# Group 1's attention scores by query, and part of the late rotation on VectorE, in a transformer block of fp32 products

## The reference

```python
h = ada_rms(x, time_emb, ln1_w, ln1_tw)          # x * rsqrt(mean(x^2)) * w * (1 + t @ tw.T)
q, k, v = h @ Wq.T, h @ Wk.T, h @ Wv.T           # 8 query heads, 1 key/value head of 32
q, k = apply_rope(q, pos_ids), apply_rope(k, pos_ids)   # q * cos + rotate_half(q) * sin
attn = softmax(einsum('bkgsd,bktd->bkgst', qg, k) / sqrt(32))
x = x + (attn @ v) @ Wo.T
h = ada_rms(x, time_emb, ln2_w, ln2_tw)
out = x + (silu(h @ Wg.T) * (h @ Wu.T)) @ Wd.T   # 1024 inner features
```

## Time and profile before

| | us |
|---|---|
| median of three runs (111.22, 111.94, 111.80) | 111.80 |
| profiled execution, time | 111.32 |
| its span | 109.5 |
| TensorE busy | 102.8 (94%) |
| VectorE busy | 70.2 (64%) |
| ScalarE busy | 50.5 (46%) |
| GpSimd busy | 61.9 (57%) |
| TensorE's granted clock, every 5 us of the span | 1.00 |

### The profile page before, as it was taken

One profiled execution on the slowest core, in us unless ns is written; L12 is line 12 of the kernel. 1 busy time (PEld: TensorE's weight loads), 2 busy tenths in 40 slices (PEclk: granted clock), 3 DMA queues, 4 the chain that ended last, 5 costly groups with the idle time before them and its releaser, 6 DMA issues. The chain is left out here.

```text
span 109.5 us, 2352 instructions
## 1 busy us (share of the span) xinstructions
PE 102.8 (94%) x748; PEld 95.4 (87%) x748; DVE 70.2 (64%) x176; ACT 50.5 (46%) x136; POOL 61.9 (57%) x92
## 2 busy tenths in 40 slices
PE   5979989999998999998999989999999999999990
PEld 4858758769898999988999979999999999999990
DVE  1476976889999947347998435479984354666311
ACT  5082868778626365213662326145524522444300
POOL 1006696399899979968189982252552410555500
DMA  2899999700000000000020000000200000200011
GB/s 72 141 354 411 293 363 416 313 4 6 0 0 3 6 0 0 0 0 9 0 96 0 0 0 6 3 0 0 96 6 0 0 0 0 99 6 0 0 48 48
DMA packets 3707, 7.66 MB, mean 70 GB/s; under 512 B 624, under 2 KB 1648, under 8 KB 3696
## 3 DMA queue, kind: packets, MB, share of 16 engines
q1 hardware_dynamic: 3552, 7.51, 20.0%
q10 hardware_dynamic: 144, 0.01, 0.1%
HBM read 6.47 MB, written 1.05 MB: 69 GB/s over the span
## 5 line engine op out<-in xcount | busy, mean ns | idle before, releaser
L1104 POOL TENSOR_TENSOR hf_l<-hf,hf_h 128x256 fp32r<-128x256 f32 x32 | 24.0, 751 | 24.4 <-ACT hf_h L985 24.4
L415 PE MATMUL ps_gu<-h_h,wgu_h 128*128 128x256 f32 x120 | 25.2, 291 | 0.0
L415 PE MATMUL ps_gu<-h_h,wgu_l 128*128 128x256 f32 x120 | 23.9, 280 | 0.0
L415 PE MATMUL ps_gu<-h_l,wgu_h 128*128 128x256 f32 x120 | 23.9, 280 | 0.0
L978 ACT ACTIVATE th<-ps_gu 128x256 f32<-128x256 f32 x32 | 12.2, 381 | 23.3 <-PE ps_gu L415 22.9
L764 DVE SCALAR_TENSOR_TENSOR sg<-th,ps_gu 128x256 f32<-128x256 f32 x32 | 13.2, 411 | 11.9 <-ACT th L978 11.6
L415 PEld LDWEIGHTS ps_gu<-h_h,wgu_h 128*128 128x128 f32 x120 | 18.8, 188 | 0.3
L985 ACT ACTIVATE hf_h<-hf 128x256 fp32r<-128x256 f32 x32 | 13.2, 412 | 11.4 <-DVE hf L773 11.3
L415 PEld LDWEIGHTS ps_gu<-h_l,wgu_h 128*128 128x128 f32 x120 | 18.4, 188 | 0.0
L415 PEld LDWEIGHTS ps_gu<-h_h,wgu_l 128*128 128x128 f32 x120 | 18.3, 188 | 0.0
L773 DVE TENSOR_TENSOR hf<-sg,ps_gu 128x256 f32<-128x256 f32 x32 | 13.5, 420 | 1.0
(11 more groups left out here) (142 smaller groups left out, 198.3 us busy)
## 6 DMA issues: line engine op xcount, KB each, us to landing
wgu<-in_w_gu SPq DMA_DIRECT2D x4, 512.0 KB, 9.4
xt<-in_xT SPq DMA_DIRECT2D x4, 256.0 KB, 6.6
wd<-in_w_d SPq DMA_DIRECT2D x2, 512.0 KB, 12.6
out_x<-xk SPq DMA_DIRECT2D x3, 256.0 KB, 2.2
pb<-in_pack_b SPq DMA_DIRECT2D x1, 576.0 KB, 6.2
xk<-in_x_tok SPq DMA_DIRECT2D x2, 256.0 KB, 8.1
xk<-in_x_tok SPq DMA_DIRECT2D x1, 512.0 KB, 11.5
wqkv<-in_w_qkv SPq DMA_DIRECT2D x1, 320.0 KB, 5.3
```

Of the source, the lines that this page charges most:

```text
L415: mm = pe.matmul(ps_gu[:, slot % RING, part, cols], w[:, m, span(part * KH + k, 1, P)], h[:, k, cols], start=(step == 0 and k == 0), stop= ...
L1104: pool.tensor_tensor(hf_l[:, m], hf[:, m], hf_h[:, m].bitcast(F32), ALU.subtract).then_inc(hf_lo, 1)
```

## The change

Group 1's scores are computed by query, as group 0's are: the turned form and VectorE's flip stay for groups 2 and 3 alone. With that TensorE turns group 1's `prob` (four transposes between chunks 4 and 5) and ScalarE copies it, where VectorE turned it. For groups 2 and 3 VectorE forms `rot_a` and the sum `qk_rot`, between `low_x2` and `turn_qk` at the end of stages 0 and 1; GpSimd keeps `rot_b`. In the first attention `spread_v` goes ahead of tile 1's maximum, and ScalarE's copy of `probT` ahead of `high_gu(1)`. In stages 1 and 2 chunk 6's product (`hidden`) goes ahead of the attention sum.

```diff
@@ TensorE
-                    if g:
+                    if g > 1:
                         mm = pe.matmul(bank_s(g, c0, n)[:, span(c, 1, HG * P)], keys, qkT[:, c, 0:HG * P],
...
             def turn_probs(g, c, n):
                 pe.wait_ge(prob_ready, done(g, c, n))
-                if c:
+                if g:
+                    pe.wait_ge(h2_lo, CT * g)
+                elif c:
                     pe.wait_ge(below_ready, c)
...
             gate_up(0, 4)
+            turn_probs(1, 0, CT)
             gate_up(0, 5)
@@ VectorE
-                return by_row(flip[:, :] if g else bank_s(g, c, n)[:, span(c, n, HG * P)])
+                return by_row(flip[:, :] if g > 1 else bank_s(g, c, n)[:, span(c, n, HG * P)])
...
+            def late_rotate_a(g):
+                ts = slice(g * CT, (g + 1) * CT)
+                dve.wait_ge(table_ready, 3 * (g - 1))
+                q = qkv_sb[:, ts, 0:QK].rearrange("p c (h d) -> p c h d", d=HD)
+                a = rot_a[:, :, :].rearrange("p c (h d) -> p c h d", d=HD)
+                dve.tensor_tensor(a, q, cos[:, ts].rearrange("p t u d -> p t (u d)").unsqueeze(2)
+                                  .broadcast_to([P, CT, HEADS + 1, HD]), ALU.mult).then_inc(late_a, 1)
+
+            def late_add(g):
+                dve.wait_ge(late_b, 2 * (g - 1))
+                dve.wait_ge(late_a, g - 1)
+                dve.wait_ge(qkT_ready, CT * g)
+                dve.wait_ge(kbd_ready, CT * g)
+                dve.tensor_tensor(qk_rot[:, :, :], rot_a[:, :, :], rot_b[:, :, :], ALU.add).then_inc(late_qk, 1)
...
             take_below(0, 0, 1)
+            spread_v(0, 0)
+            spread_v(0, 1)
             take_max(0, 1, 1)
             take_below(0, 1, 1)
-            spread_v(0, 0)
-            spread_v(0, 1)
...
-                flip_scores(a)
-                if g:
-                    take_max(a, 0, CT)
-                    take_below(a, 0, CT)
+                if g:
+                    flip_scores(a)
+                take_max(a, 0, CT)
+                take_below(a, 0, CT)
                 gated(g, 2)
                 hidden(g, 2)
...
-                else:
-                    take_max(a, 0, CT)
-                    take_below(a, 0, CT)
                 gated(g, 3)
                 hidden(g, 3)
                 if g == 0:
-                    turn_probs(a)
                     low_down(2)
...
                 gated(g, 6)
-                if g == 0:
-                    hidden(g, 6)
+                hidden(g, 6)
                 add_attention(a, 0)
-                if g:
-                    hidden(g, 6)
                 add_attention(a, 1)
...
                 if b < GROUPS:
+                    late_rotate_a(b)
+                    late_add(b)
                     turn_qk(b, 0, CT)
@@ ScalarE
             def copy_probT(g, c, n):
                 act.wait_ge(probT_ps, done(g, c, n))
+                if g:
+                    act.wait_ge(ctx_ready, CT * g)
...
             exps(0, 0, 1)
+            copy_probT(0, 0, 1)
             high_gu(1)
-            copy_probT(0, 0, 1)
             exps(0, 1, 1)
...
                 tanh(g, 2)
-                if g:
-                    exps(a, 0, CT)
+                exps(a, 0, CT)
                 tanh(g, 3)
+                high_hidden(g, 2)
                 if g == 0:
-                    exps(a, 0, CT)
-                high_hidden(g, 2)
-                if g and b < GROUPS:
+                    copy_probT(a, 0, CT)
+                elif b < GROUPS:
@@ GpSimd
-            def late_rotate_a(g): ...
-            def late_add(g): ...
...
             low_hidden(0, 7)
-            late_rotate_a(2)
-            late_add(2)
             spread_k(2)
...
                 low_hidden(g, 4)
-                if b < GROUPS:
-                    late_rotate_a(b)
                 low_hidden(g, 5)
-                if b < GROUPS:
-                    late_add(b)
                 low_hidden(g, 6)
```

More of the change, by code:

```diff
@@ L679, in take_max @@
             def take_max(g, c, n):
-                if g:
-                    dve.wait_ge(flip_ready, g)
+                if g > 1:
+                    dve.wait_ge(flip_ready, g - 1)
                 else:
@@ L1148, in late_rotate_b @@
                                    ALU.mult).then_inc(late_b, 1)
[L1150 to L1162, removed]
             def first_spread_k(c):
```

## The result

| us | before | after |
|---|---|---|
| median (five runs each) | 111.80 | 110.42 |
| profiled execution, time | 111.32 | 110.94 |
| its span | 109.5 | 109.2 |
| first mean square on TensorE starts | 7.17 | 8.04 |
| from there to the end of the span | 102.33 | 101.16 |

What follows compares the result with a forecast made beforehand. TensorE, busy 94% of the span, was taken as the bound, with its few waits. The terms -0.20 + 0.0 - 1.61 + 0.50 gave -1.31 us, so 110.3 us from a mean of 111.57; 8-in-10 range 109.5 to 111.5.

Steps and rivals of the forecast that it cites:

- A: First attention, values' spread ahead and ScalarE reordered: context 0.50 us earlier, partly lost behind `high_gu(1)`; -0.20 us, bounds -0.50 and 0.
- B: Group 1 by query: transposes +0.50, scores +0.05, `probT` wait gone -0.57; sum 0.0 us, bounds -0.2 and +0.35.
- C: Group 2's rotation on VectorE: the `kbd` wait at its scores goes, margin 0.57 us; with D -1.61 us.
- D: Group 1's down products: less on GpSimd and chunk 6's product ahead end the `hf_l` wait; with C -1.61 us.
- E: Group 3's rotation on VectorE: scores 0.41 us late, a new wait; +0.50 us, bounds 0.25 and 1.9.
- drain and refill: TensorE's pipeline at a wait: each costs about 0.25 us more than the profile shows.
- The port: SBUF port shared by VectorE's new operations and GpSimd: no cost in the sum; late side would pay at most one low part.
- rival 1: Better than forecast: no wait at group 3's scores, whole 0.50 us kept in first attention; -2.1 us, chance 0.15.
- Rivals 2, 3 and 4: Group 1's hand-off late (-0.74 us, chance 0.12); down product's wait stays (-0.56, 0.08); port contended (-0.6, 0.07).
- rival 5: Slower: VectorE's 576-element rotation operations take 1.43 us each at groups 2 and 3; +0.88 us, chance 0.08.

Runs made afterwards that it cites:

- after_again: The changed kernel run again unedited, on the chip of the follow-up runs; median 110.33 us, ratio to the kernel before 0.9875.
- e1: Changed kernel with group 3's rotation product back on GpSimd, only its sum on VectorE; median 109.88 us, ratio to the kernel before 0.9822.
- e8: Changed kernel with group 3's rotation product on GpSimd and `high_gu(1)` back ahead of the `probT` copy; median 110.09 us, ratio to the kernel before 0.9845.
- e9: The kernel of e8 with GpSimd spreading group 1's keys tile by tile; median 109.38 us, ratio to the kernel before 0.9792.
- e2: Changed kernel with both rotation products and both sums back on GpSimd; median 111.27 us, ratio to the kernel before 0.9961.
- e3: Changed kernel with chunk 6's product of stages 1 and 2 back behind the first attention sum; median 110.36 us, ratio to the kernel before 0.9866.
- e7: Changed kernel with VectorE's rotation product done twice for groups 2 and 3; median 111.19 us, ratio to the kernel before 0.9971.
- e4_turned: Changed kernel with group 1 turned as before: VectorE's flip and turn, no transposes, no copy; median 110.53 us, ratio to the kernel before 0.9903.
- e5: Changed kernel with ScalarE's `high_gu(1)` back ahead of the copy of tile 0's `probT`; median 109.99 us, ratio to the kernel before 0.9895.

## Why the prediction was right, step by step

The forecast of -1.31 us came out as -1.38 by the medians, and as -1.17 and -1.32 by the bodies of two profiles. The ratio of 0.9892 stands for 1.2 us (0.8 to 1.6): the 113.72 us in the five runs before lifts their median, and part of the agreement of -1.31 with -1.38 is luck.

- **A**, -0.20 forecast: -0.11 and -0.23 in two profiles, -0.14 in the mean of six. The context came 0.46 earlier (0.50 forecast), and the exp behind `high_gu(1)` took most of it back, as the sum had it.
- **B**, 0.0: from group 1's scores to chunk 6, 35.86 - 29.37 = 6.49 us against 6.56. The four transposes took 0.36 to the next start, and chunk 5's first product 0.08 more than its like: 0.44 for my 0.50. The hand-off had the order I gave it but a smaller margin: in after_again the copy ended at 33.60 and the context began at 34.17, 0.57 for my 0.7.
- **C and D**, -1.61: stage 1 shrank by 1.54. The missing 0.07 is an assumption of the sum: stage 1 without any wait lasts 21.06 us and stage 2 without any 20.98 (e1, e8, e9), so the two waits cost 1.53 of the difference of 1.61. Where the 0.08 comes from is open. C's wait is gone with a margin of 0.67 (0.57 forecast). D's cause was the sum on GpSimd; the change's other half, the product ahead, was given a part in the working and has none (e2, e3).
- **E**, +0.50: stage 2 grew by 0.48 and 0.52. The two operations took 0.75 and 0.76 (0.77 forecast). e1 and e7 show the cause from both sides: 0.84 us less on VectorE takes the wait away, 0.78 more adds 0.80. The scores stood 3.22 us behind the stage's first product, 0.40 late (0.41 forecast), with 0.24 listed and 0.48 paid. So the 0.25 that the prediction adds "for drain and refill" is mostly the gap between what is listed and how late the start is (0.60 and 0.76 at 49.73 before); on top of the lateness this wait cost 0.08, and the fuller 0.66 would have counted that gap twice. Drain and refill as its cause no run shows.
- **The port.** The rotation products on VectorE ran at 0.75 with no GpSimd work beside them, so the rule of the Trainium skill (SBUF — State Buffer, Who interferes with whom), that a VectorE operation with two SBUF inputs contends with a GpSimd one that reads SBUF, was not put to the test at this place. At the down weights it was. e4_turned, which has the old order of group 1, has the long subtraction of the earlier trace rows again; in the changed kernel VectorE is done before GpSimd begins, and GpSimd's takes 1.29. The delay is 0.45 us in the kernel before (0.44 in e4_turned), less than the 0.60 (0.58) for which VectorE's operation still ran. The lines are first e4_turned's, then the changed kernel's:

```profile
35.77 0.67 DVE L799 TENSOR_TENSOR wd_l<-wd,wd_h 128x512 fp32r<-128x512 f32 x1
35.86 1.73 POOL L1138 TENSOR_TENSOR wd_l<-wd,wd_h 128x512 fp32r<-128x512 f32 x1
```

```profile
33.89 0.71 DVE L800 TENSOR_TENSOR wd_l<-wd,wd_h 128x512 fp32r<-128x512 f32 x1
35.41 1.29 POOL L1134 TENSOR_TENSOR wd_l<-wd,wd_h 128x512 fp32r<-128x512 f32 x1
```

- The gains of rival 1 exist, but in e5 and e1 and not in the changed kernel. Rivals 2, 3 and 4 did not happen, and rival 5 had the right place and the wrong duration.

Left open: whether A is 0.1 or 0.2, since that stretch varies by 0.16 us among six profiles with the same code there.

## What to carry to other kernels

Where one engine is nearly always busy, price a wait by two stages of equal work and not by what the profile lists: here 1.10 us listed cost 1.5 to 1.6. Work that moves from a loaded engine to an idle one is free only if that one has slack before TensorE's next product: the same two operations cost nothing at group 2, where 0.67 us of slack stood behind them, and 0.5 us at group 3, where there was none, and splitting them over both engines took that away too. When a start has room, move the one instruction that is late, and leave the rest of the order: the second swap of the first attention took back more than half of what the first gave (0.19 of 0.33 us by the traces).

## What the runs showed of the hardware

The landing of the first x moved TensorE's first mean square between 7.11 and 8.04 us with the same transfers, a spread of 0.9 us of the time (0.8%) that is chance. On VectorE, 576 elements out of SBUF in an order of 9 heads by 32, with one input repeated over the heads, took 0.75 us, hardly more than 512 plain ones (0.69); GpSimd took 1.44 for the same (e1_mixed).

GpSimd's 128x512 subtraction of the down weights took 1.74 us (before) and 1.73 (e4_turned) where it began 0.08 and 0.09 us behind VectorE's subtraction of the same size, and 1.27 to 1.29 in the ten other profiles, where VectorE's was over before it began.
